# Graph layer on one core: transposed node rows over x, a ring of 96 gathered tiles, and products ahead of transposes in the first chunks

## What is computed

```python
h = jnp.maximum(_layernorm(x, axis=-1), 0.0)
row, col = (edge_index[0], edge_index[1])
m_in = jnp.concatenate([h[row], edge_attr], axis=1)
messages = jax.nn.relu(m_in @ msg_w1 + msg_b1) @ msg_w2 + msg_b2
aggregated = jax.ops.segment_sum(messages, col, num_segments=x.shape[0])
u = jax.nn.relu(jnp.concatenate([h, aggregated], axis=1) @ upd_w1 + upd_b1)
return x + (u @ upd_w2 + upd_b2)
```

## Time and profile before

| what | value |
|---|---|
| median of 3 runs | 4671.3 us (4669.88 to 4673.83) |
| span of the profiled execution | 4668.9 us |
| TensorE (matmuls) busy | 2500.6 us, 54% |
| VectorE busy | 1914.8 us, 41% |
| GpSimd busy | 2954.6 us, 63% |
| ScalarE busy | 138.6 us, 3% |
| DMA, mean over the span | 73 GB/s, of it gathers 205 MB |

### The profile page before, as it was taken

The page is one execution under the profiler, slowest core; times in us unless marked ns, Lnnn a source line. Parts: engine busy times, 40 slices in busy tenths (PEclk is TensorE's granted clock), DMA queues, the critical chain, the costliest instruction groups (busy, mean ns, idle before and its releaser), DMA issues.

```text
span 4668.9 us, 32312 instructions
## 1 busy us (share of the span) xinstructions
PE 2500.6 (54%) x10696; PEld 2151.4 (46%) x10696; DVE 1914.8 (41%) x1990; ACT 138.6 (3%) x257; POOL 2954.6 (63%) x3133
## 2 busy tenths in 40 slices
PE   1557555555555555555555555555555555545455
PEld 1357544444444444444444444444444444444444
DVE  1546534334344343343343343443443433444444
ACT  1520000000000000000000000000000000000000
POOL 6345666666666666666666666666666666666665
PEclk6777766666676676666666666666767667676676
DMA  4312222222222222222222222222222222233322
GB/s 112 126 49 82 78 67 71 67 67 71 67 67 71 67 67 71 67 65 72 67 71 67 67 71 67 67 71 67 67 71 67 65 72 67 75 100 97 87 77 59
DMA packets 154626, 340.77 MB, mean 73 GB/s; under 512 B 73896, under 2 KB 74920, under 8 KB 154188
## 3 DMA queue, kind: packets, MB, share of 16 engines
q0 software_dynamic: 100000, 205.00, 16.7%
q1 hardware_dynamic: 46165, 121.97, 8.2%
q10 hardware_dynamic: 8406, 13.14, 0.9%
HBM read 327.06 MB, written 12.81 MB: 73 GB/s over the span
## 4 chain that ended last, share of the span: by engine, by line
issue 41%; PE 36%; DVE 7%; POOL 6%; another core or an unknown queue 6%; DMA 1%; ACT 1%; DVEq 1%; ACTq 0%; SPq 0%; POOLq 0%
PE pre L487 20%; PE seg L540 13%; POOL x_all L403 4%; POOL rows L403 2%; DVE h_space L1021 2%; DVE x_all L967 1%; DVE rows L967 1%; PE spare L555 1%; PE spare L556 1%; DVE space L1007 1%; DMA rows<-table,index 1%; DMA x_all<-table,index 1%; PE pre L508 0%; DVEq L1046 0%
## 5 line engine op out<-in xcount | busy, mean ns | idle before, releaser
L487 PE MATMUL pre<-w_attr_sb,attrs 128*128 128x256 f32 x3126 | 1332.7, 598 | 1309.7 <-issue 1206.9
L403 POOL DMA_INDIRECT rows<-table,index x1509 | 1427.8, 946 | 868.1 <-issue 532.4
L403 POOL DMA_INDIRECT x_all<-table,index x1536 | 1450.0, 944 | 801.1 <-issue 516.6
L487 PEld LDWEIGHTS pre<-w_attr_sb,attrs 128*128 128x128 f32 x3126 | 905.8, 304 | 1574.1 <-issue 1280.6
L967 DVE TENSOR_TENSOR x_all<-pre,x_all 128x1024 f32<-128x1024 f32 x192 | 234.9, 1224 | 1181.7 <-DMA x_all<-table,index 1155.1
L967 DVE TENSOR_TENSOR rows<-pre,rows 128x1024 f32<-128x1024 f32 x189 | 230.8, 1221 | 1081.9 <-DMA rows<-table,index 1058.9
L540 PE MATMUL seg<-space,rows 128*128 128x80 f32 x3178 | 482.6, 302 | 284.5 <-issue 283.7
L540 PEld LDWEIGHTS seg<-space,rows 128*128 128x128 f32 x3178 | 491.8, 227 | 302.2 <-issue 279.6
L540 PE MATMUL seg<-space,x_all 128*128 128x80 f32 x3072 | 479.7, 308 | 282.4 <-issue 281.9
L540 PEld LDWEIGHTS seg<-space,x_all 128*128 128x128 f32 x3072 | 491.7, 234 | 285.4 <-issue 262.1
L1021 DVE TENSOR_REDUCE h_space<-space 128x240 f32<-128x1920 f32 x130 | 438.6, 3374 | 0.0
(11 more groups left out here) (82 smaller groups left out, 597.6 us busy)
## 6 DMA issues: line engine op xcount, KB each, us to landing
attrs<-in_attr SPq DMA_DIRECT2D x130, 768.0 KB
x_all<-table,index POOLq DMA_INDIRECT x1536
rows<-table,index POOLq DMA_INDIRECT x1509
table<-rows SPq DMA_DIRECT2D x20, 224.0 KB
h_space<-in_x ACTq DMA_DIRECT2D x13, 224.0 KB
out<-h_space ACTq DMA_DIRECT2D x13, 224.0 KB
x_all<-in_x ACTq DMA_DIRECT2D x12, 224.0 KB
out<-x_all ACTq DMA_DIRECT2D x12, 224.0 KB
```

Source lines behind the costliest of these rows:

```text
L403: pool.indirect_dma_start(slot_rows(j)[:, t, :], None, source, bass.IndirectOffsetOnAxis(index[0:EDGES, j, t:t + 1], 0))\
L487: return pe.matmul(columns(j, q, PAIR)[:, two * 2 * D:(two + 1) * 2 * D], attrs[:, j % 2, start:start + EDGES], w_attr_sb[:, :], start=Tru ...
```

## The change

Six edits. The ring of gathered tiles keeps only the four blocks in `rows` (96 tiles), and the first leads are capped at 12. The transposed node rows are written over `x_all`, in node order: VectorE's copy writes 16 bytes apart, the weight loads for the table read 16 bytes apart, the update product reads and writes contiguous columns, and so does ScalarE's L717. VectorE's wait for the update product of five groups earlier goes. TensorE's node loop is written out (four bodies in place of a loop). In the early chunks the products of chunk s come ahead of the transposes of chunk s+1. SyncE's wait for the last update product goes; ScalarE waits for the stores of `table_first` before it loads x again, since the second x buffer now lies there.

```diff
@@ -18,9 +18,10 @@
 PAIRS = 3
 TILES_B = PAIRS * PAIR
 SLOTS = 8
+RING = 4
 AHEAD = 5
 LEAD = 3
-FIRST_LEADS = {3: 16, 4: 16, 5: 16, 6: 16, 7: 16, 8: 14, 9: 10, 10: 7}
+FIRST_LEADS = {3: 12, 4: 12, 5: 12, 6: 12, 7: 12, 8: 12, 9: 10, 10: 7}
 WINDOW = 80
 WIDE = 256
 EARLY = 3
@@ -112,6 +113,7 @@
 
         x_all = sb("x_all", [P, J * D])
         x_nodes = x_all[0:NP, :].rearrange("p (g r d) -> p g r d", g=GROUPS, r=ROWS)
+        h_all = x_all[:, 0:N]
         update = sb("update", [P, PADDED])
 
         dst_rel = sb("dst_rel", [P, max(DT * EDGES, ALL_TILES)])
@@ -123,8 +125,7 @@
         span_int = sb("span_int", [1, 1], I32)
 
         index = sb("index", [P, SLOTS, TILES_B], I32)
-        rows = sb("rows", [P, SLOTS // 2, TILES_B, D])
-        rows_late = x_all[:, 0:SLOTS // 2 * TILES_B * D].rearrange("p (s t d) -> p s t d", s=SLOTS // 2, t=TILES_B)
+        rows = sb("rows", [P, RING, TILES_B, D])
         attrs = sb("attrs", [2 * K_ATTR, 2, PAIRS * COLUMNS])
 
         NODE = UNROLL * ROWS
@@ -146,8 +147,8 @@
         h = h_space[0:NP, :].rearrange("p (k r d) -> p k r d", k=UNROLL, r=ROWS)
         h_early_t = h_space[:, 0:PAIR * P].rearrange("p (t e) -> p t e", t=PAIR)
         u = h_space[:, 0:ROWS * NP].rearrange("f (r p) -> f r p", r=ROWS)
-        x_final = [h_space[0:NP, ROWS * D:2 * ROWS * D].rearrange("p (r d) -> p r d", r=ROWS),
-                   x_all[0:NP, (J - ROWS) * D:J * D].rearrange("p (r d) -> p r d", r=ROWS)]
+        table_first = sb("table_first", [P, ROWS, D])
+        x_final = [h_space[0:NP, ROWS * D:2 * ROWS * D].rearrange("p (r d) -> p r d", r=ROWS), table_first[0:NP]]
         spot = 2 * ROWS * D
         base_row = h_space[0:1, spot:spot + (BLOCKS + 1) * BASES].bitcast(I32)
         spot += (BLOCKS + 1) * BASES
@@ -156,10 +157,7 @@
         spot += 2 * PAIRS * WINDOW
         mask_sum = h_space[0:EDGES, spot:spot + 2 * PAIRS * WINDOW].rearrange("p (s w) -> p s w", s=2)
         assert PAIR * P <= 2 * ROWS * D and WIDE <= 2 * PAIRS * WINDOW
-        h_t = attrs[:, :, :].rearrange("p s e -> p (s e)")[:, 0:UNROLL * ROWS * NP].rearrange("p (k e) -> p k e", k=UNROLL)
-
-        table_first = sb("table_first", [P, ROWS, D])
-        table_rest = rows[0:NP, SLOTS // 2 - 1].rearrange("p t d -> p (t d)")[:, PAIR * D:PAIR * D + (UNROLL - 1) * ROWS * D]\
+        table_rest = rows[0:NP, RING - 1].rearrange("p t d -> p (t d)")[:, PAIR * D:PAIR * D + (UNROLL - 1) * ROWS * D]\
             .rearrange("p (k r d) -> p k r d", k=UNROLL - 1, r=ROWS)
         table_out = [table_first[0:NP]] + [table_rest[:, k] for k in range(UNROLL - 1)]
 
@@ -279,7 +277,11 @@
 
         def slot_rows(j):
 
-            return rows[0:EDGES, j] if j < SLOTS // 2 else rows_late[0:EDGES, j - SLOTS // 2]
+            return rows[0:EDGES, j % RING]
+
+        def h_group(g):
+
+            return h_all[:, bass.ds(g * GROUP, GROUP)]
 
         def block_of(i, j):
 
@@ -377,8 +379,6 @@
                     need(sp, summed, b * PAIRS + (PAIRS - (SLOTS - AHEAD) * PAIRS))
                     load_index(*nxt)
                 load_attr(i, j)
-
-            sp.wait_ge(update_ready, after(GROUPS - 1))
             for j in range(SLOTS):
                 load_block(0, j)
             with sp.Fori(1, ROUNDS) as i:
@@ -455,11 +455,11 @@
                 pe.wait_ge(h_t_made, after(g))
                 pe.wait_ge(table_made, after(g, BACK[k]))
                 for r in range(ROWS):
-                    last = pe.matmul(seg[0:NP, k % 2, r * D:(r + 1) * D], h_t[:, k, r * NP:(r + 1) * NP],
+                    last = pe.matmul(seg[0:NP, k % 2, r * D:(r + 1) * D], h_group(g).rearrange("f (p r) -> f r p", r=ROWS)[:, r, :],
                                      w_src_sb[:, :], start=True, stop=True)
                 last.then_inc(table_ready, 1)
                 pe.wait_ge(update_made, after(g, BACK[k]))
-                pe.matmul(pre[:, k % 2, 512:512 + ROWS * NP], w_node_sb[:, :], h_t[:, k, :],
+                pe.matmul(pre[:, k % 2, 512:512 + GROUP], w_node_sb[:, :], h_group(g),
                           start=True, stop=True).then_inc(update_ready, 1)
 
             def node_groups(i, last):
@@ -469,7 +469,7 @@
                     node_products(i * UNROLL + k, k)
 
             turn_h(0, 0)
-            with pe.Fori(0, GBODIES - 1) as i:
+            for i in range(GBODIES - 1):
                 node_groups(i, False)
             node_groups(GBODIES - 1, True)
 
@@ -620,9 +620,9 @@
                     return
                 turn_early(*steps[0])
                 for s, (j, q) in enumerate(steps):
+                    early_products(j, q)
                     if s + 1 < len(steps):
                         turn_early(*steps[s + 1])
-                    early_products(j, q)
                     if s >= 1:
                         hidden_sums(0, *steps[s - 1])
                         if steps[s - 1][1] == 0:
@@ -714,8 +714,7 @@
 
                 act.wait_ge(update_ready, after(g))
                 act.sem_inc(act_turns, 1)
-                act.activation(update[:, bass.ds(g * GROUP, GROUP)].rearrange("f (p r) -> f r p", r=ROWS),
-                               pre[:, k % 2, 512:512 + ROWS * NP].rearrange("f (r p) -> f r p", r=ROWS), ACT.Identity,
+                act.activation(update[:, bass.ds(g * GROUP, GROUP)], pre[:, k % 2, 512:512 + GROUP], ACT.Identity,
                                bias=b_upd1_col[:, :]).then_inc(update_made, 1)
 
             def node_groups(i, last):
@@ -792,6 +791,7 @@
                     act.wait_ge(out_stored[(g - 1) % 2], 16 * len(CUT) * ((g - 1) // 2 + 1))
                     load_x(g + 1)
 
+            act.wait_ge(table_stored[0], 16 * len(CUT) * GBODIES)
             load_x(0)
             load_x(1)
             for g in FINISH:
@@ -860,8 +860,8 @@
             def h_t_out(g, k):
 
                 dve.wait_ge(h_turned, after(g))
-                dve.wait_ge(update_ready, after(g, UNROLL))
-                dve.tensor_copy(h_t[:, k, :], pre[:, k % 2, 0:ROWS * NP]).then_inc(h_t_made, 1)
+                dve.tensor_copy(h_group(g).rearrange("f (p r) -> f r p", r=ROWS), pre[:, k % 2, 0:ROWS * NP].rearrange("f (r p) -> f r p", r=ROWS))\
+                    .then_inc(h_t_made, 1)
 
             def table_rows_out(i, k, first):
                 if not first:
```

## The result

The changed kernel takes 4645.2 us (median of 14 runs, 4623.7 to 4662.5) where the kernel before, run beside it, takes 4666.9 us (4655.2 to 4677.8): a ratio of 0.9948, 95% interval 0.9932 to 0.9964, some 24 us less by the ratio (22 by the medians). The forecast was 4664 with a range of 4640 to 4688: the sign and the range held, the gain is about three times the forecast 7 us.

What follows compares the result with a forecast made beforehand. The prediction took the rate at which gathers are served, plus time with none waiting, to bound the kernel. Ring and order -9.2 and node stage +2 gave -7.2 on 4668.9, 4661.7; with the median 2.4 above the span, 4664 us, range 4640 to 4688.

Steps and rivals of the forecast that it cites:

- a backlog grows: Steady part: GpSimd issues gathers faster than the 1.452 us each is served; its 5 us waits drain what has piled up.
- 34.85 us a block: Steady part: time from one block's first gather to the next one's, read as 1.452 us per gather and expected unchanged.
- So service paces: Chunks 12 to 20: eight gathers take 11.62 us, plus 1.1 us idle, 12.7 us a step; chunk 20 at 319.7.
- service: The pace at which gathers are served, 1.452 us each, taken to limit the steady part and the early chunks.
- 1.46 us of idle service in each step: Kernel before, chunks 16 to 23: steps of 13.08 us against 11.62 for eight gathers, the rest set by the early chain.
- The node stage: Before the table gathers: ScalarE's L717 shortens, VectorE's spaced copy lengthens and becomes the bound; +2 us, between -5 and +8.
- I take them as hidden: Node stage: spaced weight loads, four a group, add 0 to +0.43 or +1.05 us a group, covered by TensorE's spare time.
- rival C: Node stage: spaced weight loads add 1.05 us a group, net +16, 4687 us; decides from 370 ns per load; chance 0.15.
- B: Ramp: no lead binds after chunk 12, chunk 33 starts 40 us earlier, 4633 us; chance 0.15.
- D: Ramp: the change shifts nothing, idle time comes back at the next lead; 4671 us, chance 0.20, of it 0.02 slower.
- the ledger: Start of chunk 33: ring and order costed by idle gather time; chunk 27 9.2 us earlier, passed on to the end.

Runs made afterwards that it cites:

- order alone: Kernel before with only the early chunks' products of a chunk put ahead of the next chunk's transposes: ratio 0.9970 to the kernel before.
- ring alone: Kernel before with only the ring of 96 tiles and first leads capped at 12: ratio 0.9964 to the kernel before.
- the pair of one occasion: Kernel before and changed kernel, both unedited, traced again on one occasion: ratios 0.9996 and 0.9945, spans 4659.2 and 4631.0 us.
- ring_order: Kernel before with the smaller ring, capped first leads and new early order, without the node part: ratio 0.9936, median 4637 us.

## Why the prediction was right, and where its sizes were off

**The frame held.** The early sum that waited for 48 gathers waits for 16: it stands at 249.45 with order alone and at 206.47 with ring alone. So it is the number of gathers issued ahead, not the order of the products, that sets when VectorE hears of chunk 0. The mechanism behind it is not the one that the prediction gave: "a backlog grows" is not so of the transfers, which had landed 2.6 us after their issue where the lines show it (chunk 102), and what the 1.44 us are stays open. Its 34.85 us a block were one block; 44 blocks of that trace average 34.78, and those of every other trace with a lead of 3 34.6. The earlier sum is not gained as such: with ring alone it comes 43 us earlier and chunk 24 only 7.5 us earlier. What counts are the steps behind it: with ring alone chunks 12 to 20 still take (324.48 - 221.23)/8 = 12.9 us each, with ring and order 12.0 and in the changed kernel 11.7. In the pair of one occasion the shift at chunk 33 passes to the end one to one, and the steady block is unchanged.

**The step whose size failed: "So service paces, plus the 0.8 us for the signal at least and 1.46 as before at most; I take 1.1, the middle, as neither end has a nearer row: 12.7 us a step."** Chunks 12 to 20 take (315.61 - 221.70)/8 = 11.74 us a step, and the service of eight gathers at 34.58/24 is 11.53: 0.2 us idle a step (0.4 in ring_order), not 1.1. The bound from below was too high. A reading of this, argued and not shown: if the chain of an early chunk is shorter than the service, GpSimd hears of the sum while gathers are still being served, and the time of the signal is hidden; it costs only where the chain is the longer one. The chain starts shorter than I had it: with the products ahead, the first three sums are 6.5 us apart (two of them, of ring_order, stand below), where I had 8.5 from TensorE's durations behind a stretch with a granted clock of 0.55; in the changed kernel the same stretch has 0.88 (the windows above).

```profile
205.95 1.23 DVE L961 TENSOR_TENSOR rows<-pre,b_msg_bc 128x1024 f32<-128x1024 f32 x1 [2.12 <-PE pre L508]
212.49 1.23 DVE L961 TENSOR_TENSOR rows<-pre,b_msg_bc 128x1024 f32<-128x1024 f32 x1 [1.55 <-PE pre L508]
```

Behind them the sums are held back with the gathers: from the fourth (227.53) to the tenth (305.62) they are 13 us apart on average.

By size: chunk 12 came 35.6 us after the first table gather (forecast 37.6), the eight steps 93.9 us (101.7), chunks 20 to 24 47.3 us (47.5). So of the 10 us by which the forecast for chunk 24 was too late, 8 are this gap.

**Order alone** by the same step: I expected 0 to 3 us, since only the 1.46 us of idle service in each step were to shrink a little. It brought 14. The steps fell by 1.1 us each, and chunk 24 gains 11.8 us.

**The node stage: +2 forecast, +6.2 and +6.9 measured** (first table gather 186.56 against 180.37, 186.09 against 179.18). "I take them as hidden" was wrong of the weight loads. I counted four a group; 116 in 14.5 groups are eight. Eight loads by 0.134 us are 1.07 us a group, TensorE had 0.24 to spare by my own sum, and the loads overlap matmuls only in part. The other sizes were right: L717 0.677 us (forecast 0.72), the spaced copy L863 (L864 before) 1.073 (1.07, by the ratio of the earlier trace rows). So rival C's mechanism decided this stage, at 322 ns below its point of 370, and too cheaply to decide the sign. The two errors have opposite signs, a ramp 10 us too slow and a node stage 4 to 5 us too cheap, and so hide each other in part: that the time still fell into the range is in part luck.

The Trainium skill (Advanced Engine Details and Errata, section SBUF Cachelines) asks for two hits on a line of 16 bytes. The weight loads agree (1.71 times as long at one float per line), and so does the moving operand. By this rule the node part would make the stage longer; it did, by 6 us.

**The other rivals.** B (no lead binds) did not come: chunk 27 still waits 9.15 us and chunk 33 21.40 in the second trace of the changed kernel. D (the shift is lost at the next lead) fits one pair of traces and not the other: counted from the first table gather, the 18.6 us at chunk 24 are 35.0 at chunk 33 in the pair of one occasion, but in the first traces 20.6 us shrink to 7.6. Against D stands the total time of 12 executions of each kernel or more, 22 to 26 us less on both occasions. Behind chunk 24 the waits are not steady. From chunk 24 to 33 the kernel before took 126.1 and 143.5 us, the changed kernel 139.1 and 127.1: no sign, and 12 to 17 us of scatter. Single executions of the changed kernel, 4624 to 4663 us, spread by 39.

**What stays open.** 19.6 us at chunk 24 less 6.5 in the node stage make 13; the ratios say 22 to 26, with intervals from 16 to 35. Whether the other 9 to 13 us (3 at the lower end of the intervals) are made between chunk 24 and 33, where two traces of each kernel scatter too much to say, was not settled. Nor was it settled what paces the gathers at 1.44 us, and why signals and TensorE's instructions come late while many have been issued.

## What to carry to other kernels

Where a stream of gathers sets the pace, count the time in which it stands idle, not the idle time of engines: here the ledger found both parts of the gain, though not their sizes. A constant pace does not say what paces: look when each transfer lands and what the other engines do meanwhile before calling it a rate of the DMA. A long lead is not free: what is fetched ahead and not consumed must be worked off at the end, so try leads one by one (on ring_order 3, 4, 6 and 12 gave 4637, 4625 and 4620, 4635 and 4649 us; of these only the intervals of 4 and 12 lie apart). Before a difference between two traces is explained, take both kernels once more on one occasion, since a steady block 0.6% longer than all others belonged to the occasion here.

## What was not expected of the hardware

- With 48 gathers issued, VectorE's first sum came 45.6 us after TensorE had finished its operands, and some 6 us after the DMA engines had moved the last row; with 16 gathers VectorE had been idle for 1.5 and 2.1 us before it (the sums above). With a lead of 12 chunks, waits of 20 and 31 us that the trace calls remote stand in the steady part, at an unchanged block of 34.5 us, and TensorE's instructions come 0.70 us apart or a multiple of it before the longer one.
- A moving operand that lies 500 bytes apart costs TensorE about as much, in proportion, as spaced weights: 1020 in place of 584 ns, at a granted clock of 1.00 in this stretch.
- Two executions of the same kernel differ by 17 us in nine chunks of the ramp (126.1 and 143.5 us), while the steady block is the same within 0.1% in all traces of the study with a lead of 3, the first of before apart.
